# Attention stage of a four-stage layer: decayed scores become the stationary operand, values stream, and the residual is summed by tokens

## The chip, the cores and the metric

One core of a Trainium2 chip. The metric is the device time of the program in microseconds, as the median of its runs; lower is better. Each core has TensorE (PE, with its weight loads shown apart as PEld), VectorE (DVE), ScalarE (ACT), GpSimd (POOL) and SyncE (SP), which issues the DMAs.

## The reference, cut to what matters

Four residual steps over 1024 tokens (4 batches of 256) of 256 features: `x = x + A(layernorm(x))`, `x = x + FFN(layernorm(x))`, `x = x + B(layernorm(x))`, `x = x + FFN(layernorm(x))`. The change lies in B and in the two norms around it. B has 16 heads. For one head, with 128 key features and 256 value features:

```python
q = silu(group_conv(h @ Wq.T)); k = silu(group_conv(h @ Wk.T)); v = h @ Wv.T
beta = sigmoid(h @ Wb.T + bb); gate = sigmoid(h @ Wg.T + bg)
S_t = beta_t * S_(t-1) + k_t v_t^T          # scan over the 256 tokens of a batch
o_t = (q_t S_t) * gate_t
out = concat_over_heads(o) @ Wo.T
```

The scan equals a masked product within a batch: o = M V, with M[l, m] = (q_l . k_m) times a decay for m <= l, and zero otherwise.

## The kernel before, in words

All of it is one hand-ordered program: each engine has its own list of instructions, in program order, and waits on counting semaphores. x lies in SBUF by features: `x[p, k, token]`, 128 partitions of features, two feature halves k (KT = 2), 1024 tokens. The normed input `xn` has the same layout. Every product is made from pairs of fp32r parts, hi and lo, by `mm3` (L241 to L245): three matmuls into the same place of PSUM, w.hi v.hi, w.hi v.lo, w.lo v.hi, each with a weight load of its own. The hi part is a copy on ACT (L389), the lo part a subtraction on POOL (L393) or DVE.

A norm (`norm_pe`, `norm_act`, `norm_dve`) runs before each stage: means by a matmul of x with a constant matrix (L294), x minus mean on DVE (L376), squares on ACT, variances by matmuls (L301), the inverse root on DVE, its spread over partitions by a matmul (L310), the scaling on DVE and the hi/lo split. `keep_busy` (L316) issues matmuls of zeros so that PE doesn't fall silent.

Stage B (`b_pe`, `b_act`, `b_dve`, `b_pool`, `b_sp`) goes over 16 heads. The value and output weights are multiplied first ("fold"), so that a head's contribution to x is M (xn fold) and no output projection follows. While head h is finished, head h + 1 is made. PE's order in one head (`b_head_pe`): fold and the two projections of q and k of head h + 1; scores of batches 0 and 1; values of head h + 1 (8 blocks of tokens, 48 matmuls); **value product of batch 0**; scores of batches 2 and 3; **value product of batch 1**; the two convolutions of head h + 1 (72 matmuls); **value products of batches 2 and 3**. The last head makes nothing.

For one batch the score product s has keys m on partitions and queries l on columns; only three of its four 128x128 blocks are kept, as 384 columns (TRI): [keys 0, queries 0], [keys 1, queries 1], [keys 0, queries 1]. DVE bounds the exponents (L707), ACT takes the exponentials (L713, L714), DVE multiplies them with the scores (`b_score_dve`, m_b, L1496), ACT and POOL split the result into `ms_b` hi and lo. Then `b_value_pe` makes the head's part of x, by features:

```python
for d in range(KT):
    mm3(half_view(o[:, d*SEQ:(d+1)*SEQ]), v block 0 [:, dv], first_m(ms), ...)   # 256 columns
    mm3(o[:, d*SEQ+P:(d+1)*SEQ], v block 1 [:, dv], ms[:, P:2P], ...)            # 128 columns
```

The first argument after the output is the stationary operand, the second the moving one. `b_value_dve` adds the bank to x (L1502, 128x512). The PSUM banks: 6 and 7 for the value products, 4 and 5 for the scores, 3 for the fold, 0, 1, 2 and 4 for the convolutions. In the convolutions, PE's second one (s = 1) waits for DVE to have read the banks of the first (`b_conv_y`, L1471 to L1476), and DVE does so behind the last `m_b` of the head. In rows of the profile a matmul is named by its moving operand, then its stationary one: `ps<-ms_b_hi,vtok_hi` is a value product of before, with `vtok` stationary.

## Time and profile before

| | |
|---|---|
| median of 3 runs (lowest, highest) | 1497.19 us (1496.82, 1499.1) |
| the profiled execution | 1496.01 us |
| its span, first to last instruction | 1494.2 us |
| mean granted TensorE clock | 0.989 of full |
| PE busy, instructions | 1437.9 us (96%), x8520 |
| DVE, ACT, POOL busy | 897.2, 863.9, 817.1 us |
| stage B | about 703.8 us (first mean of its norm) to 1226.7 us (first mean of the next norm) |

How to read it: a timeline row gives start, duration, engine, line, operation, output<-inputs, partitions x columns and count, and in brackets how long the engine sat idle before it and what released it. A PE matmul's own duration includes its way through the array, so what a matmul costs in a stream is the distance from its start to the start of the next, called the pitch below.

### The profile page before, as it was taken

How to read it: one execution, taken by the hardware profiler on the slowest of the kernel's cores; microseconds unless marked ns; L12 is line 12 of the kernel's file. 1: busy time of each engine (PE TensorE's matmuls, PEld its weight loads, DVE VectorE, ACT ScalarE, POOL GpSimd, SP SyncE). 2: the span in 40 equal slices, each digit the busy share in tenths (PEclk: the TensorE clock that was granted, in tenths of full speed). 3: DMA queues.
4: the chain of work that ended last, by engine and by line, in shares of the span. 5: the costliest groups of instructions: out<-in, count | busy, mean ns of one | idle time of the engine just before them, and what ended most of it. 6: DMA issues, size and time to landing. Idle time of an engine off the chain costs nothing.

```text
span 1494.2 us, 24410 instructions
## 1 busy us (share of the span) xinstructions
PE 1437.9 (96%) x8520; PEld 1248.1 (84%) x8520; DVE 897.2 (60%) x1713; ACT 863.9 (58%) x1735; POOL 817.1 (55%) x685
## 2 busy tenths in 40 slices
PE   7799999999999999999999999999999999999998
PEld 5589898898976778887789999999999987778886
DVE  6776766767664443434766767677666754443434
ACT  5566666666655343333677777777777755343332
POOL 4744444444434555553576666766676634555553
PEclk9999999999999999999999999999999989999999
DMA  2133332332311111111232123212222011111111
GB/s 83 32 66 79 68 69 67 67 78 68 69 53 32 43 43 53 42 53 32 65 82 63 51 57 74 63 49 56 63 63 63 15 42 33 43 42 53 42 53 39
DMA packets 48603, 82.48 MB, mean 55 GB/s; under 512 B 4256, under 2 KB 29984, under 8 KB 48288
## 3 DMA queue, kind: packets, MB, share of 16 engines
q1 hardware_dynamic: 48544, 81.70, 21.1%
q8 instruction: 36, 0.59, 0.2%
q14 instruction: 23, 0.19, 0.0%
HBM read 80.38 MB, written 1.31 MB: 55 GB/s over the span
## 4 chain that ended last, share of the span: by engine, by line
PE 58%; issue 5%; ACT 5%; DVE 4%; POOL 4%; DMA 0%; DVEq 0%; POOLq 0%; ACTq 0%; SPq 0%
PE ps L243 19%; PE ps L245 18%; PE ps L244 18%; POOL planes_lo L393 1%; POOL ms_b_lo L393 1%; ACT q L1317 1%; POOL qk_lo L393 1%; PE ps L294 1%; PE ps L301 1%; DVE qsum L1455 1%; ACT planes_hi L1322 1%; DVE f_h L1081 0%; DMA fw_raw<-ffn_w 0%; ACT qk_hi L389 0%; ACT fh_hi L389 0%
## 5 line engine op out<-in xcount | busy, mean ns | idle before, releaser
L393 POOL TENSOR_TENSOR ms_a_lo<-m_a,ms_a_hi 128x384 fp32r<-128x384 f32 x128 | 129.9, 1015 | 200.2 <-ACT ms_a_hi L389 200.2
L1081 DVE TENSOR_TENSOR f_h<-f_sc,ps 128x512 f32<-128x512 f32 x112 | 76.4, 682 | 182.5 <-POOL f_sc L1013 182.5
L243 PE MATMUL ps<-xn_hi,fgu_hi 128*128 128x512 f32 x448 | 177.3, 396 | 5.2 <-DVE f_h L1081 5.2
L245 PE MATMUL ps<-xn_hi,fgu_lo 128*128 128x512 f32 x448 | 178.2, 398 | 0.0
L244 PE MATMUL ps<-xn_lo,fgu_hi 128*128 128x512 f32 x448 | 177.0, 395 | 0.0
L1083 DVE TENSOR_TENSOR fh_lo<-f_h,fh_hi 128x512 fp32r<-128x512 f32 x112 | 107.2, 957 | 98.3 <-ACT fh_hi L389 98.3
L962 ACT ACTIVATE f_s<-ps 128x512 f32<-128x512 f32 x112 | 66.7, 597 | 161.2 <-PE ps L245 161.0
L1013 POOL TENSOR_TENSOR f_sc<-f_s,coef_r 128x512 f32<-128x512 f32 x88 | 114.0, 1296 | 67.5 <-ACT f_s L962 67.5
L389 ACT CAST fh_hi<-f_h 128x512 fp32r<-128x512 f32 x112 | 69.1, 617 | 124.9 <-DVE f_h L1081 124.8
L393 POOL TENSOR_TENSOR fd_lo<-fw_raw,fd_hi 128x256 fp32r<-128x256 f32 x56 | 52.1, 930 | 125.7 <-ACT fd_hi L389 125.7
L243 PE MATMUL ps<-xn_hi,aw_hi 128*128 128x512 f32 x256 | 108.8, 425 | 7.4 <-DVE bmat_lo L696 7.4
L744 DVE TENSOR_TENSOR m_a<-ps,e_a 128x384 f32<-128x384 f32 x128 | 71.4, 558 | 63.5 <-ACT e_a L714 47.4
L393 POOL TENSOR_TENSOR ms_b_lo<-m_b,ms_b_hi 128x384 fp32r<-128x384 f32 x64 | 64.8, 1013 | 78.8 <-ACT ms_b_hi L389 78.8
L243 PEld LDWEIGHTS ps<-xn_hi,fgu_hi 128*128 128x128 f32 x448 | 84.3, 188 | 27.9 <-issue 6.0
L393 POOL TENSOR_TENSOR qk_lo<-qf,qk_hi 128x512 fp32r<-128x512 f32 x64 | 84.1, 1335 | 36.5 <-ACT qk_hi L389 36.5
L245 PE MATMUL ps<-xn_hi,aw_lo 128*128 128x512 f32 x256 | 102.0, 399 | 0.0
L244 PE MATMUL ps<-xn_lo,aw_hi 128*128 128x512 f32 x256 | 101.6, 397 | 0.0
L244 PEld LDWEIGHTS ps<-xn_lo,fgu_hi 128*128 128x128 f32 x448 | 84.1, 188 | 20.5
L245 PEld LDWEIGHTS ps<-xn_hi,fgu_lo 128*128 128x128 f32 x448 | 84.2, 188 | 20.1
L243 PE MATMUL ps<-fh_hi,fd_hi 128*128 128x512 f32 x224 | 89.0, 397 | 0.6 <-DVE fh_lo L1083 0.6
L244 PE MATMUL ps<-fh_lo,fd_hi 128*128 128x512 f32 x224 | 88.2, 394 | 0.0
L245 PE MATMUL ps<-fh_hi,fd_lo 128*128 128x512 f32 x224 | 87.2, 389 | 0.0
(276 smaller groups left out, 4901.1 us busy)
## 6 DMA issues: line engine op xcount, KB each, us to landing
fw_raw<-ffn_w SPq DMA_DIRECT2D x56, 384.0 KB, 3.0
rows_a<-a_rows_d SPq DMA_DIRECT2D x64, 256.0 KB, 4.8
wconv_raw<-b_conv SPq DMA_DIRECT2D x16, 513.0 KB, 3.6
aw_raw<-a_heads SPq DMA_DIRECT2D x32, 256.0 KB, 5.2
wvo_raw<-b_vo SPq DMA_DIRECT2D x16, 512.0 KB, 3.6
rows_b<-b_rows_d SPq DMA_DIRECT2D x32, 256.0 KB, 4.8
wqk_raw<-b_qk SPq DMA_DIRECT2D x16, 256.0 KB, 4.8
x<-xT SPq DMA_DIRECT2D x2, 512.0 KB, 4.9
```

What stands on the lines that cost most here:

```text
L243: nc.tensor.matmul(o, w[0], v[0], start=first, stop=False, skip_group_check=True)
L244: nc.tensor.matmul(o, w[0], v[1], start=False, stop=False, skip_group_check=True)
L245: return nc.tensor.matmul(o, w[1], v[0], start=False, stop=last, skip_group_check=True)
L294: ins = nc.tensor.matmul(ps[:, mean_bank(n) + c, :], mean_w[:], x[:, k, cols(c)], start=k == 0, stop=k == KT - 1)
L301: ins = nc.tensor.matmul(ps[:, 2 + c, i:i + 1], ln_sq[:, k, block_of(c, i)], mean_w[:, 0:1], start=k == 0 and i == 0, stop=k == KT - 1 and ...
L389: return nc.scalar.copy(dst[0], src).then_inc(sem(hi_sem), 1)
L393: return nc.gpsimd.tensor_tensor(dst[1], src, f32(dst[0]), ALU.subtract).then_inc(sem(done_sem), 1)
L744: nc.vector.tensor_tensor(m_a[:, u % 2, :], ps[:, 4 + u % 2, 0:TRI], e_a[:, u % 2, :], ALU.mult).then_inc(sem("a_m_done"), 1)
L962: nc.scalar.activation(f_s[:, c], ps[:, c, :], ACT.Silu).then_inc(sem("f_silu"), 1)
L1013: nc.gpsimd.tensor_tensor(f_sc[:, c], f_s[:, c], coef[:, cols(c)], ALU.mult).then_inc(sem("f_sc"), 1)
L1081: nc.vector.tensor_tensor(f_h[:, c], f_sc[:, c], ps[:, 2 + c, :], ALU.mult).then_inc(sem("f_h"), 1)
L1083: nc.vector.tensor_tensor(fh[1][:, p, cols(c)], f_h[:, c], f32(fh[0][:, p, cols(c)]), ALU.subtract).then_inc(sem("f_h_split"), 1)
```

## The change

In each of the 64 value products (16 heads, 4 batches) the operands change places: `ms_b` is stationary and `vtok` moves, 256 columns wide. The output then has tokens on partitions and features on columns, so one batch's part takes 3 `mm3` (9 matmuls of 256 columns) where it took 4 (6 of 256 columns and 6 of 128). x must have the same layout while it is summed. So within the norm ahead of stage B, after the means, PE turns x over: 4 batches of 4 transposes each into banks 4 to 7, and DVE copies batches 0 and 1 back over x, ACT batches 2 and 3. In the last head PE turns each batch back after its value product has been added (turn 0 ahead of value 2, turn 1 ahead of value 3, turns 2 and 3 behind it), and DVE copies each one back. `x_final` of the norm behind the stage waits for these copies (`x_turned`) where it waited for the additions. PE's zero matmuls in the norm ahead of stage B go to bank 0 instead of 4. Three semaphores are merged into others, with no change of order.

```diff
--- before.py
+++ after.py
@@ -273,11 +273,13 @@
         X_FINAL = {1: lambda c: 4 * A_TILES + 2 * c + 2, 2: lambda c: 2 * c + 2,
-                   3: lambda c: BATCH * (B_HEADS - 1) + 2 * c + 2, 4: lambda c: 2 * c + 2}
+                   4: lambda c: 2 * c + 2}
         def x_final(eng, n, c):
             if n == 0:
                 eng.wait_ge(sem(f"x_loaded{c}"), 16)
+            elif n == 3:
+                eng.wait_ge(sem("x_turned"), BATCH + 2 * c + 2)
             else:
                 eng.wait_ge(sem(f"x_updated{n}"), X_FINAL[n](c))
@@ -293,6 +295,9 @@
                 for k in range(KT):
                     ins = nc.tensor.matmul(ps[:, mean_bank(n) + c, :], mean_w[:], x[:, k, cols(c)], start=k == 0, stop=k == KT - 1)
                 ins.then_inc(sem("ln_mean"), 1)
+            if n == 2:
+                for b in range(BATCH):
+                    turn_pe(b, 4 + b).then_inc(sem("x_turn"), 1)
             for c in range(CHUNKS):
                 for k in range(KT):
@@ -302,18 +307,34 @@
                                                start=k == 0 and i == 0, stop=k == KT - 1 and i == CHUNK_BLOCKS - 1,
                                                skip_group_check=True)
                 ins.then_inc(sem("ln_var"), 1)
-                keep_busy(pe, (6, 3)[c])
-            pe.wait_ge(sem("ones_made"), 1)
+                keep_busy(pe, (6, 3)[c], 0 if n == 2 else 4)
+            pe.wait_ge(sem("mean_made"), 2)
             for c in range(CHUNKS):
                 pe.wait_ge(sem("ln_diag"), CHUNKS * n + c + 1)
                 nc.tensor.matmul(ps[:, 2 + c, :], ones_w[:], ln_diag[:, c, :], start=True, stop=True).then_inc(sem("ln_rstd"), 1)
-                keep_busy(pe, 3)
-        def keep_busy(pe, n):
+                keep_busy(pe, 3, 0 if n == 2 else 4)
+        def of_turn(b):
+            return x[:, :, b * SEQ:(b + 1) * SEQ]
+        def turn_pe(b, bank):
+            for i in range(2):
+                for k in range(KT):
+                    at_ = i * DM + k * P
+                    ins = nc.tensor.transpose(ps[:, bank, at_:at_ + P], of_turn(b)[:, k, i * P:(i + 1) * P], ident)
+            return ins
+        def turned(bank):
+            return ps[:, bank, :].rearrange("p (i m) -> p i m", i=2)
+        def keep_busy(pe, n, bank):
             for _ in range(n):
-                nc.tensor.matmul(ps[:, 4, :], zero_w[:], zero_x[:], start=True, stop=True)
+                nc.tensor.matmul(ps[:, bank, :], zero_w[:], zero_x[:], start=True, stop=True)
         def block_of(c, i):
             return slice(c * CHUNK + i * P, c * CHUNK + (i + 1) * P)
@@ -330,6 +351,11 @@
             for c in range(CHUNKS):
                 act.wait_ge(sem("ln_v"), CHUNKS * n + c + 1)
                 nc.scalar.activation(norm_cols(ln_s, c), norm_cols(ln_v, c), ACT.Sqrt).then_inc(sem("ln_std"), 1)
+            if n == 2:
+                for b in range(2, BATCH):
+                    act.wait_ge(sem("x_turn"), b + 1)
+                    act.wait_ge(sem("ln_xc"), KT * CHUNKS * (n + 1))
+                    nc.scalar.copy(of_turn(b), turned(4 + b)).then_inc(sem("x_turned"), 1)
             for c in range(CHUNKS):
                 for k in range(KT):
                     act.wait_ge(sem("ln_xn"), KT * (CHUNKS * n + c) + k + 1)
@@ -375,6 +401,11 @@
                 for k in range(KT):
                     nc.vector.tensor_tensor(ln_xc[:, k, cols(c)], x[:, k, cols(c)], ps[:, mean_bank(n) + c, :],
                                             ALU.subtract).then_inc(sem("ln_xc"), 1)
+            if n == 2:
+                dve.wait_ge(sem("ln_xc"), KT * (CHUNKS * n + 1))
+                for b in range(2):
+                    dve.wait_ge(sem("x_turn"), b + 1)
+                    nc.vector.tensor_copy(of_turn(b), turned(4 + b)).then_inc(sem("x_turned"), 1)
             rstd(0)
             rstd(1)
             for c in range(CHUNKS):
@@ -808,8 +839,8 @@
                 sp.dma_start(aw_raw[:, h], a_heads[h * P:(h + 1) * P, :]).then_inc(sem(f"aw_loaded{h}"), 16)
             sp.dma_start(awo_raw[:], a_wo[0:P, :]).then_inc(sem("awo_loaded"), 16)
             sp.wait_ge(sem("a_cum"), 1)
-            sp.dma_start(a_rows_d, dec_e[:]).then_inc(sem("a_rows_stored"), 16)
-            sp.wait_ge(sem("a_rows_stored"), 16)
+            sp.dma_start(a_rows_d, dec_e[:]).then_inc(sem("rows_stored"), 16)
+            sp.wait_ge(sem("rows_stored"), 16)
             for c in range(CHUNKS):
                 sp.dma_start(rows_a[:, c], rows_of(a_rows_d, 0, c)).then_inc(sem(f"a_rows_loaded{c}"), 16)
             for g in range(A_TILES):
@@ -1096,6 +1127,7 @@
         def b_pe(pe):
             pe.wait_ge(sem("b_bg_w"), 1)
+            pe.wait_ge(sem("x_turned"), BATCH)
             for c in range(CHUNKS):
                 normed(pe, 2, c)
                 for s in range(2):
@@ -1239,13 +1271,10 @@
             elif not last:
                 pe.wait_ge(sem("v_split"), 4 * h + 5 + b)
             o, ms = ps[:, 6 + u, :], at(ms_b, slice(None), u)
-            for d in range(KT):
-                dv = slice(d * P, (d + 1) * P)
-                mm3(half_view(o[:, d * SEQ:(d + 1) * SEQ]), at(vtok[p], slice(None), 2 * b, dv), tuple(first_m(v) for v in ms),
-                    d == 0, False)
-                ins = mm3(o[:, d * SEQ + P:(d + 1) * SEQ], at(vtok[p], slice(None), 2 * b + 1, dv),
-                          at(ms, slice(None), slice(P, 2 * P)), False, d == KT - 1)
-            ins.then_inc(sem("b_o_done"), 1)
+            v0, v1 = (at(vtok[p], slice(None), 2 * b + i) for i in range(2))
+            mm3(o[:, 0:DM], at(ms, slice(None), slice(0, P)), v0, True, False)
+            mm3(o[:, DM:], at(ms, slice(None), slice(2 * P, TRI)), v0, False, False)
+            mm3(o[:, DM:], at(ms, slice(None), slice(P, 2 * P)), v1, False).then_inc(sem("b_o_done"), 1)
         def b_head_pe(pe, h, p, last):
             make = (lambda *parts: None) if last else (lambda *parts: b_make_pe(pe, h + 1, 1 - p, parts))
@@ -1258,8 +1287,15 @@
             b_score_pe(pe, h, p, 3, last)
             b_value_pe(pe, h, p, 1, last)
             make("conv0", "conv1")
+            if last:
+                b_turn_pe(pe, 0)
             b_value_pe(pe, h, p, 2, last)
+            if last:
+                b_turn_pe(pe, 1)
             b_value_pe(pe, h, p, 3, last)
+            if last:
+                b_turn_pe(pe, 2)
+                b_turn_pe(pe, 3)
         def b_prepare_act(act):
             act.wait_ge(sem("wbg_loaded"), 16)
@@ -1498,9 +1534,16 @@
         def b_value_dve(dve, h, b):
             dve.wait_ge(sem("b_o_done"), BATCH * h + b + 1)
-            at_ = (slice(None), slice(None), slice(b * SEQ, (b + 1) * SEQ))
-            nc.vector.tensor_tensor(x[at_], x[at_], ps[:, 6 + b % 2, :].rearrange("p (d l) -> p d l", d=KT),
-                                    ALU.add).then_inc(sem("x_updated3"), 1)
+            nc.vector.tensor_tensor(of_turn(b), of_turn(b), turned(6 + b % 2), ALU.add).then_inc(sem("x_updated3"), 1)
+        def b_turn_pe(pe, b):
+            pe.wait_ge(sem("x_updated3"), BATCH * (B_HEADS - 1) + b + 1)
+            turn_pe(b, b).then_inc(sem("x_turn"), 1)
+        def b_turn_dve(dve, b):
+            dve.wait_ge(sem("x_turn"), BATCH + b + 1)
+            nc.vector.tensor_copy(of_turn(b), turned(b)).then_inc(sem("x_turned"), 1)
         def b_head_dve(dve, h, p, last):
             make = (lambda *parts: None) if last else (lambda *parts: b_make_dve(dve, h + 1, 1 - p, parts))
@@ -1522,8 +1565,15 @@
             make("conv0")
             b_value_dve(dve, h, 1)
             make("conv1")
+            if last:
+                b_turn_dve(dve, 0)
             b_value_dve(dve, h, 2)
+            if last:
+                b_turn_dve(dve, 1)
             b_value_dve(dve, h, 3)
+            if last:
+                b_turn_dve(dve, 2)
+                b_turn_dve(dve, 3)
         def b_pool(pool):
             split_lo(pool, at(wbg, slice(None)), wbg_raw[:], "wbg_hi", 1, "b_bg_w")
@@ -1605,8 +1655,8 @@
                 sp.wait_ge(sem(f"{name}_split"), 1)
                 sp.dma_start(raw[:], src[P:2 * P, :]).then_inc(sem(f"{name}_loaded"), 16)
             sp.wait_ge(sem("b_row"), 1)
-            sp.dma_start(b_rows_d, bg_z[:, 1]).then_inc(sem("b_rows_stored"), 16)
-            sp.wait_ge(sem("b_rows_stored"), 16)
+            sp.dma_start(b_rows_d, bg_z[:, 1]).then_inc(sem("rows_stored"), 16)
+            sp.wait_ge(sem("rows_stored"), 32)
             for c in range(CHUNKS):
                 sp.dma_start(rows_b[:, c], rows_of(b_rows_d, 0, c)).then_inc(sem(f"b_rows_loaded{c}"), 16)
             with sp.Fori(0, B_HEADS - 2) as h:
@@ -1659,7 +1709,7 @@
         @block.vector
         def _(dve):
             nc.vector.memset(mean_w[:], 1.0 / DM).then_inc(sem("mean_made"), 1)
-            nc.vector.memset(ones_w[:], 1.0).then_inc(sem("ones_made"), 1)
+            nc.vector.memset(ones_w[:], 1.0).then_inc(sem("mean_made"), 1)
             a_early_dve(dve)
             dve.wait_ge(sem("consts_loaded"), 16)
             nc.vector.memset(zero_w[:], 0.0)
```

## Rows read from the trace of the kernel before

**Rows 1.** The page, part 1: busy time, share of the span and instructions of each engine.

```profile
PE 1437.9 (96%) x8520; PEld 1248.1 (84%) x8520; DVE 897.2 (60%) x1713; ACT 863.9 (58%) x1735; POOL 817.1 (55%) x685
```

**Rows 2.** Windows: stretch, length, busy (count) by engine, granted clock, DMA share, GB/s.

```profile
827.00:858.00 31.00, 30.27 (x230) 28.96 (x231) 21.81 (x47) 23.68 (x46) 20.74 (x17) 1.00 0.22 59
...
718.00:720.00 2.00, 2.00 (x6) 1.58 (x6) 2.00 (x2) 1.38 (x2) 2.00 (x2) 0.53 0.02 6
...
1216.00:1218.00 2.00, 2.00 (x11) 2.00 (x11) 0.00 (x0) 0.42 (x1) 1.00 (x1) 0.50 0.00 0
```

**Rows 3.** The chain of waits, 844 to 858: start, us, what.

```profile
847.32 0.59 ACT q L1317
...
855.43 0.57 DVE m_b L1496
...
856.61 1.02 POOL ms_b_lo L393
```

**Rows 4.** Timeline of PE: the first value product of two heads following each other.

```profile
827.10 0.38 PE L243 MATMUL ps<-ms_b_hi,vtok_hi 128*128 128x256 f32 x1 [0.64 <-POOL ms_b_lo L393]
...
857.75 0.38 PE L243 MATMUL ps<-ms_b_hi,vtok_hi 128*128 128x256 f32 x1 [0.64 <-POOL ms_b_lo L393]
```

**Rows 5.** Timeline of PE, 840 to 845: value products, then the fold.

```profile
840.76 0.33 PE L243 MATMUL ps<-ms_b_hi,vtok_hi 128*128 128x256 f32 x1
...
841.17 0.22 PE L243 MATMUL ps<-ms_b_hi,vtok_hi 128*128 128x128 f32 x1
841.23 0.28 PE L244 MATMUL ps<-ms_b_lo,vtok_hi 128*128 128x128 f32 x1
...
841.45 0.34 PE L243 MATMUL ps<-ms_b_hi,vtok_hi 128*128 128x256 f32 x1
...
842.84 0.34 PE L243 MATMUL ps<-wvo_hi 128*128 128x256 f32 x1
...
844.31 0.40 PE L243 MATMUL ps<-xn_hi,wqk_hi 128*128 128x512 f32 x1
```

**Rows 6.** Timeline of DVE and of PE, 832 to 836, the first convolution.

```profile
832.80 0.56 DVE L1496 TENSOR_TENSOR m_b<-ps,e_b 128x384 f32<-128x384 f32 x1 [1.25 <-ACT e_b L714]
833.78 0.43 DVE L1471 COPY conv_y<-ps 128x256 f32<-128x256 f32 x1 [0.42 <-PE ps L245]
...
835.04 0.42 DVE L1476 TENSOR_TENSOR conv_y<-conv_y,ps 128x256 f32<-128x256 f32 x1
...
835.72 0.28 PE L243 MATMUL ps<-planes_hi,wconv_hi 128*128 128x260 f32 x1
```

**Rows 7.** Timeline of ACT, 844 to 848.

```profile
844.51 0.59 ACT L1309 CAST fold_hi<-ps 128x512 fp32r<-128x512 f32 x1 [0.18 <-PE ps L245]
...
847.32 0.59 ACT L1317 COPY q<-ps 128x512 f32<-128x512 f32 x1 [0.69 <-PE ps L245]
```

**Rows 8.** Timeline of PE, 66 to 67: eight transposes of an earlier stage.

```profile
66.07 1.06 PE L491 MATMUL ps<-const,stage 128*128 128x128 f32 x8
66.89 0.48 PE L243 MATMUL ps<-xn_hi,aw_hi 128*128 128x512 f32 x1
```

**Rows 9.** Timeline of ACT and of PE, the norm ahead of stage B.

```profile
714.63 1.21 ACT L336 CAST xn_hi<-ln_xc 128x512 fp32r<-128x512 f32 x2 [2.16 <-DVE ln_xc L364]
...
717.77 0.50 PE L243 MATMUL ps<-xn_hi,wbg_hi 128*128 128x512 f32 x1 [1.94 <-POOL wbg_lo L393]
```

**Rows 10.** Timeline of PE and DVE, the last head and the norm behind it.

```profile
1212.26 0.36 PE L243 MATMUL ps<-qk_hi 128*128 128x256 f32 x1 [1.82 <-POOL qk_lo L393]
...
1215.73 0.58 PE L243 MATMUL ps<-ms_b_hi,vtok_hi 128*128 128x256 f32 x1 [1.37 <-POOL ms_b_lo L393]
...
1225.31 0.39 PE L243 MATMUL ps<-ms_b_hi,vtok_hi 128*128 128x256 f32 x1 [0.37 <-POOL ms_b_lo L393]
...
1226.73 3.65 PE L294 MATMUL ps<-x,mean_w 128*128 128x512 f32 x8
1226.94 0.69 DVE L1502 TENSOR_TENSOR x<-x,ps 128x512 f32<-128x512 f32 x1 [1.27 <-PE ps L245]
```

## The prediction

> **What bounds the kernel now.** The page's busy times come first: PE is busy for 96% of the span and its weight loads for 84%, every other engine for at most 60% [rows 1]. A window over one head of stage B shows the same at full clock: PE 30.27 of 31 us, the weight loads 28.96, ACT 23.68 [rows 2]. Then the waits of PE. In this stage the one that comes back in every head stands ahead of the first value product, 0.64 us, released by the lo split of `ms_b` on POOL [rows 4]; the heads follow each other at 857.75 - 827.10 = 30.65 us. 14 such waits are there (the last of them 0.47 us, the others 0.63 or 0.64).
>
> A wait of 0.64 us doesn't say that POOL bounds the head, so the chain of waits is read next [rows 3]. From the first value product (827.10) to the end of the first q projection (about 847.3) the chain is PE alone. There it goes over to ACT (847.32), and through ACT, DVE and POOL by turns until POOL's split at 856.61, which releases PE. This second part, 847.32 to 857.75 = 10.43 us, is a latency that PE's work beside it (projections, scores, values) doesn't fill. So a head is 20.2 us bound by PE and 10.4 us bound by a round trip. What the reader must check is where the changed matmuls lie. All four value products of a head lie between its first one and the next fold, so all lie in PE's part.
>
> **The value products.** In the stream of before, 840.76 to 841.45 is half a batch: three matmuls of 256 columns and three of 128, 0.69 us [rows 5]. The first of the narrow ones has a pitch of 0.06, the other two 0.11, and the next wide one 0.17 where a wide one costs 0.118 otherwise: the fold's twelve take 844.31 - 842.84 = 1.47, less the 0.17 of the first, over eleven. So narrow matmuls cost (0.69 - 3 x 0.118) / 3 = 0.112 us each, almost as much as the wide ones: half the columns buy nothing, since the weight load sets the pace of a narrow matmul and only just not that of a wide one. The change keeps the columns (6 x 256 + 6 x 128 = 9 x 256 = 2304) and drops 3 of 12 weight loads. A batch falls from 2 x 0.69 = 1.38 to 9 x 0.118 = 1.06 us, so by 0.32, and a head by 1.28. Bounds: 1.38 - 9 x 0.112 = 0.37 saved if the narrow price held for all, and 6 x 0.118 + 6 x 0.06 - 1.06 = 0 if columns alone counted. I take 0.32, since the new stream is of the fold's shape, a measured row. DVE's addition keeps its shape, 128x512 from one bank, 0.69 us [rows 10].
>
> The Trainium skill, in TensorE: Matmul & The Clock Gate, section Back-to-back issue gap, gives about 81 ns for a matmul of 128 columns within a stream of weight loads and matmuls. By that a batch of before would be 6 x 0.118 + 6 x 0.081 = 1.19 us and the saving 0.13. The rows say 0.112, and they decide.
>
> **What comes late next in a head.** Seen from the first value product, batch 0 and 1 bring the convolutions 0.64 us earlier. DVE reads the first convolution's bank at 833.78 after an idle 0.42, behind `m_b` of batch 3, which ends at 832.80 + 0.56 = 833.36 [rows 6]. That `m_b` hangs on the exponents and DVE's own order, not on PE's value products (DVE is still in its value splits when product 0 is done), so it stays put. The read moves by 0.36 and not by 0.64; it ends at 835.46 - 0.36 = 835.10. PE would be at its second convolution at 835.72 - 0.64 = 835.08, and with the way of a semaphore it starts near 835.2: 0.1 lost. The second half of the convolutions has more room. Then value products 2 and 3 bring a further 0.64. On ACT the q copy that heads the chain at 847.32 sat idle for 0.69 before [rows 7]. ACT itself moves forward by about 0.55 (it follows DVE's last read) and 0.18 (the wait at 844.51). So 1.15 - 0.73 = 0.42 of the 0.69 is used and the copy is still released by PE. The 10.43 us behind it keep their length, and the wait of 0.64 stays as it is. A head saves 1.28 - 0.13 = 1.15 us. Bounds: 1.28 with no loss, 0.73 if ACT were to hold the copy back by all that the rows leave open.
>
> The 14 distances between first value products (head 0 to head 14) give 14 x 1.15 = **-16.1**. In head 14 products 0 and 1 still count, and 2 and 3 vanish in a wait: PE stands for 1.82 us ahead of the last head's scores [rows 10], released by a split that hangs on DVE's convolution read. That is **-0.5**.
>
> **The last head.** The clock is at half from about 1213 to 1223 [rows 2, 10], so a value product costs 2.6 us and saves 0.64. Product 0 is on the chain (DVE adds it before it makes the exponents of batches 2 and 3), product 1 too (the split of batch 3 waits until it has been read). That is **-1.3**. Bounds: -0.6 at full clock, -1.3 at half.
>
> **Turning x over ahead of the stage.** 16 transposes stand on PE between the means and the variances. Eight such ones, of the same type and shape, take 66.89 - 66.07 = 0.82 us, 0.103 each [rows 8]: 16 x 0.103 = 1.65. PE had no wait between means and variances, and the variances, the zero matmuls and the spread follow on PE in order, so all of it counts: **+1.7**. Bounds: 1.65 and, at half clock, 3.3. The copies: two on DVE at about 0.69 (the addition reads a bank of the same size), while DVE waits for the variances, which come 1.7 later; two on ACT at about 0.59 (as its q copy), in an idle of 2.16 [rows 9]. I take them as free. Without that cover they would cost 1.4 and 1.2. PE's new wait for the copies ahead of the gate product is long over at 717.77 + 1.7.
>
> **Turning it back.** Behind the last value product, PE was free for the means at once: 1226.73, 3.5 us for both. Now it makes turn 2, waits for DVE's last addition (0.2 + 0.69 behind the product), makes turn 3 and only then the means: 0.95 + 0.1 + 4 x 0.103 = 1.45 later. DVE's copy of batch 3 is hidden by the first mean (1.7 us). Turns 0 and 1 stand ahead of products 2 and 3: 0.4 each, 0.8 at half clock, of which the wait of 0.37 ahead of the last product [rows 10] takes a part. I take 0.9 (bounds 0.4 and 1.6). Together **+2.4**, bounds 1.8 and 3.1.
>
> **The sum**, from the profiled execution's own 1496.01 (1.8 above its span): -16.1 - 0.5 - 1.3 + 1.7 + 2.4 = -13.8, so 1482.2. The median of the runs shown is 1.2 above that execution, so 1483.4 is the forecast. DMA isn't touched: the three merged semaphores keep their order, and the weights of a head are needed 1.15 us earlier each, against landing times of a few us within a head of 29.5. With the bounds put together, 14 x 1.28 and the low ends give 1480.5, 14 x 0.73 and the high ends 1491.5.
>
> **Rivals.**
>
> A. *The round trip holds.* If ACT or DVE, not PE, releases the q copy after the change, only part of each head's 1.28 counts and the wait ahead of the first product grows instead. For it: ACT is busy for 23.68 of 31 us [rows 2] and has 0.27 left by my count. Against: the idle of 0.69 is there. At 0.73 a head the sum is 1496.01 - 10.2 + 2.3 = 1488.1, with the offset 1489.3. Chance 0.12.
>
> B. *Narrow matmuls weren't dear.* Half of the saving is an artefact of modelled starts, or the new stream is slower than the fold's. With 0.13 a batch, 0.4 a head after the convolution loss, 14 heads give 5.6, head 14 0.1, the last head 0.5, against 4.1 for the turns: 1496.0 - 2.1 + 1.2 = 1495.1. With no saving at all it is 1497.2 + 4.1 = 1501.3. Against it stand the starts themselves, which add up to the distance between heads, so no time is modelled away. This is the case in which the change doesn't do what it says. Chance 0.04, of which 0.01 with no gain at all. The skill's figure of 81 ns would lead here.
>
> C. *The clock falls at the seams.* The rows show falls after PE was thin or idle: an idle of 1.94 at 717.77 and then 0.53 of the clock [rows 2, 9], 1.82 at 1212.26 and then 0.50 for 10 us. If transposes count as such idleness, the norm ahead of the stage (14 us of PE, some of it paced by DVE) runs at half: about +5, and the means behind it (3.5 becoming 7) about +3: 1483.4 + 8 = 1491. Against: after the eight transposes at 66.07 the matmuls have full pitch, and the 15 us in which they'd lie are at 1.00 now. The skill says in TensorE: Matmul & The Clock Gate, Part 4: PE-mode transpose, that a transpose isn't counted as activity by the clock's gate; the rows have no stretch of transposes long enough to show it. Chance 0.08.
>
> D. *Slower.* The wait ahead of the first product grows to 0.64 + 1.15 = 1.8 us because the whole round trip, from the previous head's DVE work on, is what sets the head. Then no time is won, and the wait is as long as those of 1.82 and 1.94 that were followed by a half clock; at 717.77 that lasted for 3.5 us. At the shortest, each head loses 1.7 us in such a spell: 1496 + 14 x 1.7 + 4 + 1.2 = 1525. It decides from a wait of about 1.8 us on; the waits of 0.64 leave the clock at 1.00 [rows 2, 4]. Against: the chain shows PE alone ahead of 847.32. Chance 0.03.
>
> **Chances and range.** The forecast has 0.73, and its own range is 1480.5 to 1486.5. To hold 8 in 10 the range reaches to A: 1480 to 1489.5. About 0.2% (3 us) is what a measurement of this kernel can tell from no change. Faster by more than that: the forecast, A and C, 0.93; within it the larger part of B, 0.03; slower D and the rest of B, 0.04.
>
> **What would show it.** Distance between first value products 29.5 us (before 30.65), and the wait ahead of them still near 0.64. A batch of value products 1.06 us from its first matmul to the next operation, nine matmuls with a pitch of 0.118 and `vtok` named first. A wait or a gap of about 0.1 on PE at the start of the second convolution. PE instructions 8520 - 64 x 3 + 32 = 8360. 16 transposes in about 1.7 us behind the first means, and the gate product 1.7 later relative to them. Means behind the stage starting about 1.5 us after the last value product. Wrong it would be if the distance between heads were above 30 us, if the wait ahead of the first product were above 1 us, or if the granted clock fell inside the heads.

## The result, and the profile after

The changed kernel takes 1482.57 us, median of 4 runs (1481.42 to 1482.94); the kernel before, on the same chip, 1497.01 (1495.96 to 1499.1). The ratio is 0.9903 with a 95% interval of 0.9891 to 0.9914: about 14 us faster, where 1483.4 was forecast. The profiled execution took 1482.8 with a span of 1481.0, so the spans differ by 13.2.

The page of the changed kernel, its first line of busy times; it answers to [rows 1]:

```profile
PE 1420.5 (96%) x8354; PEld 1228.3 (83%) x8360; DVE 901.3 (61%) x1719; ACT 861.7 (58%) x1737; POOL 819.8 (55%) x685
```

The 8360 instructions that were counted ahead are there as weight loads (PEld), one for each matmul; six matmul records are missing from the trace. PE loses 17.4 us of busy time and stays at 96%. The copies that turn x over and back are DVE's six and ACT's two more instructions.

The timeline of PE in the changed kernel: the first batch of one head and the scores behind it; then the first product of the next head; it answers to [rows 4, 5]:

```profile
826.90 0.38 PE L243 MATMUL ps<-vtok_hi,ms_b_hi 128*128 128x256 f32 x1 [0.79 <-POOL ms_b_lo L424]
827.12 0.28 PE L244 MATMUL ps<-vtok_lo,ms_b_hi 128*128 128x256 f32 x1
...
827.93 0.28 PE L245 MATMUL ps<-vtok_hi,ms_b_lo 128*128 128x256 f32 x1
828.05 0.28 PE L243 MATMUL ps<-qk_hi 128*128 128x256 f32 x1
...
856.54 0.38 PE L243 MATMUL ps<-vtok_hi,ms_b_hi 128*128 128x256 f32 x1 [0.80 <-POOL ms_b_lo L424]
```

A batch is nine matmuls. The first of a head takes 828.05 - 826.90 = 1.15 us (its first matmul comes out of a wait and has a pitch of 0.22), where it took 1.43. The last two of the head take 839.38 to 841.48 = 2.10 together, where they took 2.72. The wait ahead of the first product has grown from 0.64 to 0.80, and that was not forecast. The distance between heads is 29.61 on the mean of fourteen, where it was 30.62.

The same spans, put into a ledger between events that both traces have (us, before, after, difference; it adds up to the 13.2). A gate product is the first product behind the norm ahead of the stage, a router product the first behind the next norm:

```
                                             before   after    diff   forecast
start -> first mean ahead of the stage       703.76  704.51   +0.75   0
first mean -> gate product                    14.01   15.75   +1.74   +1.7
gate product -> first value product, head 0   48.07   47.41   -0.66   0
heads 0 to 14 (14 distances)                 428.69  414.61  -14.08   -16.1
head 14 -> first mean behind the stage        32.20   31.61   -0.59   +0.6
first mean -> router product                  14.06   14.01   -0.05   0
the rest                                     253.41  253.10   -0.31   0
```

The first row is nothing of the change: over the profiled executions of all kernels here, which run the same work up to there, it lies between 703.64 and 705.79. So the total times of single kernels scatter by some 2 us ahead of the stage alone, and the ledger's rows within the stage say more than the totals.

### The profile page after: what moved, and what is told of

Its sections match the earlier page's. It is cut to its first block and busy times, and to the rows that moved or that the text cites. A ratio compares the mean times of both kernels' runs of the same rounds, so it can differ in the third digit from the quotient of the medians.

```text
span 1481.0 us, 24095 instructions
## 1 busy us (share of the span) xinstructions
PE 1420.5 (96%) x8354; PEld 1228.3 (83%) x8360; DVE 901.3 (61%) x1719; ACT 861.7 (58%) x1737; POOL 819.8 (55%) x685
```

## The experiments

### The two halves of the change apart

One kernel has the new value products and no turns. The value matmuls are those of the change, everything else is the kernel before:

```diff
-            for d in range(KT):
-                dv = slice(d * P, (d + 1) * P)
-                mm3(half_view(o[:, d * SEQ:(d + 1) * SEQ]), at(vtok[p], slice(None), 2 * b, dv), tuple(first_m(v) for v in ms),
-                    d == 0, False)
...
+            mm3(o[:, 0:DM], at(ms, slice(None), slice(0, P)), v0, True, False)
+            mm3(o[:, DM:], at(ms, slice(None), slice(2 * P, TRI)), v0, False, False)
+            mm3(o[:, DM:], at(ms, slice(None), slice(P, 2 * P)), v1, False).then_inc(sem("b_o_done"), 1)
```

> The value products turned round as in the change, x left by features as before (the sum over heads then mixes features and tokens): what the products give without the price of the turns. Theory (16 transposes on PE's path ahead of the stage, two turns inside the last head and two behind it, all paid): the change less 1.7 ahead of the stage and less about 2.1 at its end, 1482.6 - 3.8 = 1478.8 us; distance between heads 29.63 us as in the change. Rival 1 (the turns are hidden by the waits around them): 1482.6. Rival 2 (transposes pull the clock down): more than 6 us below the change.

Measured: 1480.75 us (1480.53 to 1480.99), ratio to the kernel before 0.9892 [0.9875, 0.9908]. The distance between heads is 29.61 and the wait 0.80, as in the change, so both belong to the products and neither to the turns. Its last head, timeline of PE from the last value product to the first mean:

```profile
1210.82 0.39 PE L243 MATMUL ps<-vtok_hi,ms_b_hi 128*128 128x256 f32 x1 [0.47 <-POOL ms_b_lo L393]
...
1211.99 1.02 PE L294 MATMUL ps<-x,mean_w 128*128 128x512 f32 x2
```

From head 14's first product to the mean it takes 30.18, the change 31.61: turning back costs 1.43. From the first value product of the last head to the mean it takes 9.57 against 11.00 before, so the cheaper products save 1.43 there (forecast 1.3). The expectation of 1478.8 was missed by 2 us: it had turns of 3.8, and between the two traces they are 1.74 + 1.43 = 3.2; 1.15 more lies ahead of the stage, where this execution came late (705.66 for 704.51).

The other kernel has the turns and the old products (the same diff the other way round, on the changed kernel).

> The reverse: x is turned over and back, the value products stay as before (the sum mixes features and tokens): the price of the turns alone. Theory: 1497.0 + 1.7 + 2.1 to 2.4 = 1500.9 us, distance between heads 30.63 us, and the gate product about 1.7 us later behind the first mean. Rival 1 (hidden): 1497.0. Rival 2 (clock): over 1503, with a granted clock below 1 in the norm.

Measured: 1499.73 (1498.53 to 1502.1), ratio 1.0023 [1.0013, 1.0032], so +3.3 us with the turns alone. The distance between heads is 30.62 and the wait 0.64, those of before. The gate product comes 15.75 behind the first mean, the 1.74 of the change. From the last head's first value product to the mean it takes 1229.55 - 1217.72 = 11.83, against 11.00 before. So turning back costs 0.83 beside the old products and 1.43 beside the new ones; no run shows why the two differ.

### Does the weight load set the price?

Each wide matmul of the change is cut into two of 128 columns: the same columns, twice the matmuls and weight loads.

```diff
-            mm3(o[:, 0:DM], at(ms, slice(None), slice(0, P)), v0, True, False)
...
+            for d in range(KT):
+                dv = slice(d * P, (d + 1) * P)
+                w0, w1 = at(v0, slice(None), dv), at(v1, slice(None), dv)
+                mm3(o[:, d * P:(d + 1) * P], at(ms, slice(None), slice(0, P)), w0, d == 0, False)
...
```

> The change with each of its 9 matmuls of 256 columns cut into two of 128: the same 2304 columns in a batch, 18 weight loads for 9. Theory (a matmul of 128 columns costs 0.112 us because its weight load sets the pace): a batch 18 x 0.112 = 2.02 for 1.06, 0.96 more; 58 batches lie on PE's part of the heads, so +56, with the last head's two at half clock +58: about 1540 us. Rival 1 (columns set the time): 1482.6 to 1486. Rival 2 (0.081 us for such a matmul, the figure of the Trainium skill): 18 x 0.081 = 1.46, +0.40 x 58 = +23: 1506 us.

Measured: 1548.05 (1547.58 to 1549.68), ratio 1.0344 [1.0327, 1.0361]. One batch in its timeline of PE, the first matmul, the fourth and the last, and the scores behind it:

```profile
834.45 0.32 PE L243 MATMUL ps<-vtok_hi,ms_b_hi 128*128 128x128 f32 x1 [0.63 <-POOL ms_b_lo L424]
...
834.83 0.28 PE L243 MATMUL ps<-vtok_hi,ms_b_hi 128*128 128x128 f32 x1
...
836.40 0.28 PE L245 MATMUL ps<-vtok_hi,ms_b_lo 128*128 128x128 f32 x1
836.51 0.33 PE L243 MATMUL ps<-qk_hi 128*128 128x256 f32 x1
```

Eighteen matmuls take 2.06 us, with a pitch of 0.11 where no neighbour is wide. Nine more matmuls with their weight loads and no more columns cost 2.06 - 1.15 = 0.91 a batch, and a head grew by 3.55 (33.16 for 29.61). So rival B is out: narrow matmuls are as dear as the rows of before had them. Still narrower ones cost almost the same. In the changed kernel, sixteen matmuls of a single column (of fp32, where the products are of fp32r) in the norm take 714.39 - 712.69 = 1.70 us, 0.106 each (timeline of PE):

```profile
712.69 1.84 PE L306 MATMUL ps<-mean_w,ln_sq 128*128 128x1 f32 x16
714.39 0.81 PE L337 MATMUL ps<-zero_x,zero_w 128*128 128x512 bf16 x3
```

So up to 128 columns it isn't the columns that are paid for. That it is the weight load, and not a fixed price of any matmul, is argued and not shown: every matmul of these kernels has a weight load of its own, and no kernel here drops one without the other.

The kernel came out 8 us above the 1540 that were expected. 14 heads make 49.6 of some 66 us; some 10 of the rest lie in the last head, at half clock. The window over the last head, the turns and the way to the means in this kernel (columns as in rows 2: length, busy by engine, granted clock, DMA share, GB/s):

```profile
1252.00:1278.00 26.00, 24.93 (x112) 23.59 (x112) 9.31 (x19) 6.16 (x14) 4.42 (x5) 0.50 0.00 1
```

PE is busy for 24.93 of 26 us at half clock. The same part, from the last head's first value product to the first mean, takes 1276.49 - 1255.09 = 21.4 here and 11.0 in the change.

### Where is a microsecond of PE worth a microsecond?

The forecast split a head into a part bound by PE and a part bound by a round trip. Two kernels put the same three matmuls on zeros (0.65 us, three of 512 columns) into the one part and into the other.

```diff
+            if not last:
+                keep_busy(pe, 3, FOLD_BANK)
             b_value_pe(pe, h, p, 2, last)      # in PE's part
...
+            if not last:
+                keep_busy(pe, 3, FOLD_BANK)
             b_value_pe(pe, h, p, 0, last)      # in the round trip's part
```

> The change with three matmuls of zeros (3 x 0.215 = 0.65 us) ahead of the value product of batch 2 in heads 0 to 14, that is in the part of the head in which the chain of waits is PE alone. Theory (what is added or taken there counts in full): 14 heads x 0.65 = +9.0, 1491.6 us; distance between heads 30.28; the wait ahead of the first value product unchanged or some 0.1 shorter. Rival (the round trip through ACT, DVE and POOL sets the head): under +3, with the wait shrinking by what is added.

> The change with three matmuls of zeros (0.65 us) ahead of the value product of batch 0 in heads 0 to 14, that is in the part of the head in which the chain goes through ACT, DVE and POOL and PE ends up waiting 0.79. Theory (PE's work there is hidden up to the length of the wait): the wait falls to about 0.15, the distance between heads stays 29.6, time as the change, a ratio to before of 0.990 to 0.991. Rival (PE's time counts wherever it stands): +9 us, 1491.

Measured: in PE's part 1490.24 (1489.39 to 1491.83), ratio 0.9954 [0.9937, 0.997]; the 14 distances are 421.05, so 6.44 longer, 0.46 a head. In the round trip's part 1484.13 (1482.07 to 1484.54), ratio 0.9911 [0.9895, 0.9928], distance 29.61: nothing. The second kernel's timeline of PE shows where the zeros went:

```profile
855.46 0.38 PE L337 MATMUL ps<-zero_x,zero_w 128*128 128x512 bf16 x1
...
855.98 0.38 PE L243 MATMUL ps<-vtok_hi,ms_b_hi 128*128 128x256 f32 x1
```

They fill the wait, of which 0 to 0.18 is left. The split of the head holds: what is added ahead of the first value product is hidden, and what is added ahead of the third is paid. But in PE's part 0.65 cost only 0.46, since the wait went back from 0.79 to 0.63. From the timeline of PE of the first kernel, the first product of two heads:

```profile
829.04 0.38 PE L243 MATMUL ps<-vtok_hi,ms_b_hi 128*128 128x256 f32 x1 [0.63 <-POOL ms_b_lo L424]
...
859.12 0.38 PE L243 MATMUL ps<-vtok_hi,ms_b_hi 128*128 128x256 f32 x1 [0.64 <-POOL ms_b_lo L424]
```

So the 0.16 that the change adds to the wait goes away when PE's part is made longer again. What meets what on the other engines is the next question.

### Who made the wait longer?

The timeline of DVE and of POOL in the changed kernel, at the head of the round trip:

```profile
847.07 0.87 DVE L1494 TENSOR_TENSOR planes_lo<-q,planes_hi 128x512 fp32r<-128x512 f32 x1 [0.83 <-ACT planes_hi L1358]
...
848.65 0.68 DVE L1494 TENSOR_TENSOR planes_lo<-q,planes_hi 128x512 fp32r<-128x512 f32 x1
```

```profile
844.67 2.73 POOL L424 TENSOR_TENSOR qk_lo<-qf,qk_hi 128x512 fp32r<-128x512 f32 x2
847.42 1.02 POOL L424 TENSOR_TENSOR planes_lo<-qsum,planes_hi 128x256 fp32r<-128x256 f32 x1
```

And in the kernel before:

```profile
848.46 0.69 DVE L1458 TENSOR_TENSOR planes_lo<-q,planes_hi 128x512 fp32r<-128x512 f32 x1 [1.19 <-ACT planes_hi L1322]
...
849.85 0.68 DVE L1458 TENSOR_TENSOR planes_lo<-q,planes_hi 128x512 fp32r<-128x512 f32 x1
```

```profile
845.70 2.72 POOL L393 TENSOR_TENSOR qk_lo<-qf,qk_hi 128x512 fp32r<-128x512 f32 x2 [0.54 <-ACT qk_hi L389]
848.81 0.84 POOL L393 TENSOR_TENSOR planes_lo<-qsum,planes_hi 128x256 fp32r<-128x256 f32 x1 [0.39 <-ACT planes_hi L1324]
```

Before, POOL was done with the lo splits of k (848.42) when DVE began its first split of the planes (848.46). After the change q comes 1.4 us sooner and POOL's splits only 1.0: they end at 847.40, and DVE's split at 847.07 runs beside them. It takes 0.87 instead of 0.69, and all behind it on DVE is 0.18 late (from split to split 1.58 instead of 1.39). The theory: POOL beside it makes DVE slow, so POOL must be done with k sooner. Three kernels test it. The first takes a large split off POOL's way to k (the lo split of the next head's window sums, which stands ahead of k in POOL's order):

```diff
-            if name == "wconv":
+            if name == "wconv" and isinstance(h, int) and h < 2:
...
                 b_weights_pool(pool, "wvo", h + 2, p)
+                b_wsum_lo_pool(pool, h + 2, p)
```

> The change, with one of POOL's jobs in a head (the lo split of the summed convolution weights, 1.3 us) moved from behind the large weight split to an idle stretch ahead of it, so that the lo split of k (2.7 us) can start earlier; nothing else is moved. Theory (the wait ahead of the first value product grew from 0.64 to 0.79 because that split of k now runs beside DVE's first instructions of the round trip, which last 0.87 instead of 0.69 us beside it): k's split is then released by ACT at about 0.1 us earlier, so only a part of the overlap goes: wait 0.70 to 0.79, time 1481.0 to 1482.5. Rival (the growth comes from ACT's or PE's own chain): wait and time unchanged, 1482.5.

Measured: 1482.94 (1481.71 to 1484.46), ratio 0.9905 [0.9889, 0.9922], to be held against the changed kernel itself, run on the same chip:

> The changed kernel itself, once more, on the chip on which the next three run: 1482.5 us, a ratio to before of 0.990, distance between heads 29.63 us and the wait ahead of the first value product 0.79.

It gave 1484.11 (1482.29 to 1485.81), ratio 0.9909 [0.9892, 0.9926]. The distance (29.61) and the wait (0.80) are the same in both: a miss, as POOL was not what k waited for any more. The timeline of POOL, early in the stage, shows why:

```profile
815.20 2.73 POOL L424 TENSOR_TENSOR qk_lo<-qf,qk_hi 128x512 fp32r<-128x512 f32 x2 [1.23 <-ACT qk_hi L420]
```

POOL now stands idle for 1.23 us until ACT has cast k, and its splits end as late as in the change (0.31 to 0.34 behind DVE's start). So ACT's order is the next thing: k's casts ahead of the fold's.

```diff
+                b_k_hi_act(act, h, p)
                 make("fold")
-                b_k_hi_act(act, h, p)
```

> The same, and on ACT the hi parts of k are made ahead of the copy of the fold, so that POOL can begin k's lo split about 0.5 us earlier and has left DVE alone when the round trip starts. Theory: DVE's first split of the round trip back to 0.69 us, wait back to about 0.64, distance between heads 29.48, 14 x 0.15 = 2.1 us less than the change: 1480.4. Rival: no gain, 1482.5, or a loss since the fold's lo part and DVE's sum of the planes come 0.3 to 0.5 us later: up to 1489.

> Only the move on ACT: the hi parts of k ahead of the copy of the fold, POOL's order as in the change. Theory (what stretched the round trip is POOL's split of k running beside DVE's first instruction of it): POOL is still busy with its weight splits until about 0.7 us after the hi part of k is there, so its split of k starts and ends as late as in the change, DVE's split still takes 0.87 us, wait 0.79, distance between heads 29.6, time as the change: a ratio of 0.990 to 0.991. Rival (the gain came from ACT's order itself): wait 0.61, distance 29.44, 0.989.

With both edits: 1481.06 (1479.35 to 1482.24), ratio 0.9889 [0.9872, 0.9905], distance 29.43, wait 0.59 to 0.63. The interval overlaps that of the changed kernel on this chip, so it is the distances that decide. Its timelines of POOL and of DVE:

```profile
843.84 2.55 POOL L424 TENSOR_TENSOR qk_lo<-qf,qk_hi 128x512 fp32r<-128x512 f32 x2 [0.76 <-ACT qk_hi L420]
```

```profile
846.71 0.69 DVE L1494 TENSOR_TENSOR planes_lo<-q,planes_hi 128x512 fp32r<-128x512 f32 x1
```

POOL ends at 846.39, ahead of DVE's 846.71, and DVE is back at 0.69. With ACT's order alone 1483.94 (1481.2 to 1484.54), ratio 0.9905 [0.9888, 0.9923], distance 29.60, wait 0.74 to 0.82:

```profile
846.72 0.90 DVE L1494 TENSOR_TENSOR planes_lo<-q,planes_hi 128x512 fp32r<-128x512 f32 x1 [0.81 <-ACT planes_hi L1358]
```

```profile
844.30 2.76 POOL L424 TENSOR_TENSOR qk_lo<-qf,qk_hi 128x512 fp32r<-128x512 f32 x2
```

POOL's splits end at 847.06 here, behind DVE's start, and DVE takes 0.90. Only where the overlap is gone is the 0.18 gone. All thirteen traces here (before, the change and the eleven runs) agree, over fourteen heads each. In seven (the change, its repeat, no turns, the early split, ACT's order alone, zeros in the round trip, zeros in the last head) POOL's splits end 0.29 to 0.37 us behind DVE's start, and DVE takes 0.85 to 0.92. In the six others (before, the turns alone, the halves, zeros in PE's part, both edits, all moves together) POOL is done first, and DVE takes 0.69.

### The clock in the last head

[rows 2, 10] showed half a clock in the last head. The changed kernel has it too, only earlier, at 1200 and not at 1213. One kernel fills PE's waits there with matmuls on zeros (2.43 ahead of the scores, 1.10 ahead of the values):

```diff
+            if last:
+                keep_busy(pe, 11, FOLD_BANK)
             b_score_pe(pe, h, p, 0, last)
             b_score_pe(pe, h, p, 1, last)
             make("values")
+            if last:
+                keep_busy(pe, 6, FOLD_BANK)
```

> The change with matmuls of zeros in the two waits of PE in the last head (11 ahead of its first scores, 2.4 us; 6 ahead of its first value product, 1.3 us). In the change the clock is at half there from 1200 to about 1207. Theory (the idle of 2.43 brings the fall): no fall, the first value product 1.06 instead of 2.09 and what hangs on it earlier, 1 to 2 us less: 1481.0. Rival (the fall comes from something else, or the zeros stand in the way of the scores): 1482.5 to 1483.5, clock still at half.

Measured: 1483.18 (1482.36 to 1484.84), ratio 0.991 [0.9893, 0.9926]. The windows in the changed kernel, then in this one:

```profile
1200.00:1202.00 2.00, 1.78 (x9) 1.59 (x8) 0.56 (x1) 1.31 (x5) 0.66 (x2) 0.50 0.03 8
1206.00:1208.00 2.00, 2.00 (x16) 2.00 (x16) 1.48 (x5) 0.88 (x3) 0.00 (x0) 0.82 0.00 0
```

```profile
1200.00:1202.00 2.00, 2.00 (x15) 1.66 (x16) 0.56 (x1) 1.30 (x5) 1.06 (x1) 1.00 0.03 8
1206.00:1208.00 2.00, 1.62 (x14) 1.38 (x13) 1.06 (x3) 1.30 (x4) 0.00 (x0) 1.00 0.00 0
```

The clock stays full, as the expectation had it, but the gain is at its low end. From head 14 to the mean it takes 30.68 against 31.61, so -0.9, which is less than the runs can tell apart in the whole time: half a clock for 7 us costs little where PE then waits for POOL (1.43 us ahead of the third value product here, 0.65 in the change).

The two gains together (three moves) give the lowest time of this study:

> The change with the three moves together: the lo split of the summed weights early on POOL, the hi parts of k ahead of the fold's copy on ACT, zeros in PE's waits of the last head. Theory (each takes away what it took away alone): distance between heads 29.44 us for 29.61, 14 x 0.18 = 2.5 less, and 0.9 less in the last head: 3.4 us less than the change, a ratio to before of 0.9875, about 1479 to 1480 us. Rival (the gains overlap or one was scatter): 1481 to 1482.

Measured: 1479.67 (1478.72 to 1480.0), ratio to the kernel before 0.988 [0.9863, 0.9896]; distance 29.42, head 14 to the mean 30.63. By its trace that is 2.72 in the 14 distances and 0.98 behind them, 3.7 below the change. By the medians it is 2.9, on different chips, and the intervals of the two ratios overlap.

## Why the prediction was right

**The sum.** -13.8 was forecast between two profiled executions, -13.2 it was. Four things were off, and they cancel, so that the sum comes this close is in part luck: heads +2.0 against the forecast, the end of the stage -1.2, the way from the gate to the first value product -0.7, and what lies outside the change +0.4. The bounds that the prediction names, put together, give 1481.0 and 1492.3, not 1480.5 and 1491.5; its range doesn't hang on that.

**The value products: right.** 1.25 us a head by the traces of one head (product 0 0.28, product 1 with the scores ahead of it 0.32, products 2 and 3 0.62, the fold 0.03) against 1.28, from four batches at 9 x 0.118. The halves kernel shows the cause: 0.91 a batch for nine more matmuls with their weight loads. The Trainium skill, TensorE: Matmul & The Clock Gate, section Back-to-back issue gap, gives about 81 ns for a matmul of 128 columns in such a stream. By that an estimate for the eighteen is 18 x 0.081 = 1.46 us; 2.06 was measured, so here the measurement decides.

**The convolutions: nearly right.** 0.1 was to be lost, 0.06 was. The timeline of DVE in the changed kernel:

```profile
832.62 0.56 DVE L1532 TENSOR_TENSOR m_b<-ps,e_b 128x384 f32<-128x384 f32 x1 [1.25 <-ACT e_b L745]
833.09 0.41 DVE L1507 COPY conv_y<-ps 128x256 f32<-128x256 f32 x1
```

As reckoned, `m_b` doesn't move against the start of the head (5.72 behind it, 5.70 before), and the read stands right behind it, without the idle 0.42 of [rows 6].

**The round trip: the step that failed.** The forecast said "The 10.43 us behind it keep their length, and the wait of 0.64 stays as it is." It is 10.61 (845.93 to 856.54). The start was right: PE, not ACT, still releases the q copy, with 0.34 of idle left where 0.27 was reckoned. The timeline of ACT:

```profile
845.93 0.59 ACT L1353 COPY q<-ps 128x512 f32<-128x512 f32 x1 [0.34 <-PE ps L245]
```

But a chain that keeps its instructions doesn't keep their durations when it moves against another engine's work. POOL's splits of k had 0.04 us of room before the change, and the forecast hadn't looked at POOL, as it isn't on that part of the chain. So the distance fell by 1.00 and not by 1.15: PE's part shortened by 1.25 - 0.06 = 1.19, and 0.18 came back in the round trip. 14 x 0.15 = 2.1 is the whole miss of the heads (2.0 by the ledger). No rival had this: A had ACT or DVE holding the copy back, and that didn't happen.

**The last head: products right, turns too dear.** The new products gave 1.43 (forecast 1.3) and head 14 gave 0.6 (forecast 0.5). The turns cost 1.43, not 2.4. The timeline of PE in the changed kernel, the last products with the turns between them:

```profile
1208.23 0.60 PE L328 MATMUL ps<-const,x 128*128 128x128 f32 x4
1209.48 0.39 PE L243 MATMUL ps<-vtok_hi,ms_b_hi 128*128 128x256 f32 x1 [0.65 <-POOL ms_b_lo L424]
...
1210.64 0.60 PE L328 MATMUL ps<-const,x 128*128 128x128 f32 x4
1211.29 0.39 PE L243 MATMUL ps<-vtok_hi,ms_b_hi 128*128 128x256 f32 x1
...
1212.45 0.60 PE L328 MATMUL ps<-const,x 128*128 128x128 f32 x4
1213.39 0.66 PE L328 MATMUL ps<-const,x 128*128 128x128 f32 x4 [0.34 <-DVE x L1537]
1213.89 1.02 PE L296 MATMUL ps<-x,mean_w 128*128 128x512 f32 x2
```

Behind the last value product it is as forecast: 1213.89 - 1212.45 = 1.44 with the wait for DVE between (1.45 reckoned). Turn 0 ends at about 1208.8 and PE still waits 0.65 for the split; turn 1 took the place of the wait ahead of the last product, which without the turns is 0.47. So the 0.9 allowed for both is 0: that term was mis-sized, and it is where the -1.2 at the end of the stage comes from, with 0.2 from the products. The half clock that the allowance was for had come and gone by then.

**Ahead of the stage: right.** 16 transposes cost 1.74 (forecast 1.65, taken as 1.7). The timeline of PE, the transposes and the variances behind them:

```profile
707.95 1.91 PE L328 MATMUL ps<-const,x 128*128 128x128 f32 x16
709.69 1.84 PE L306 MATMUL ps<-mean_w,ln_sq 128*128 128x1 f32 x16
```

That the copies are free holds too, as nothing but this 1.74 came on top.

**Rival C: the other way round.** The window over the gate products of the changed kernel; in the kernel before, that stretch had a fall of the clock [rows 2, 9]:

```profile
720.00:724.00 4.00, 3.29 (x13) 2.41 (x14) 3.91 (x8) 2.43 (x5) 4.00 (x4) 1.00 0.26 66
```

The wait of 1.94 is still there, yet the clock stays at 1.00, and from the gate product to the fold it takes 6.42 us instead of 7.24. That is 0.8 won. Behind the fold 0.16 of it is lost again: to the first value product of head 0 it takes 40.99 instead of 40.83. Both traces have a second fall of the clock there, at about 756 to 760. The windows over it in the changed kernel, and in the one with zeros in the last head, which has the same instructions up to there:

```profile
756.00:760.00 4.00, 3.98 (x10) 3.14 (x11) 3.24 (x4) 2.69 (x6) 3.20 (x4) 0.57 0.14 53
```

```profile
756.00:760.00 4.00, 2.81 (x12) 2.31 (x13) 2.75 (x4) 2.97 (x7) 3.75 (x3) 1.00 0.40 145
```

The second has no fall and takes 40.25, 0.74 less (46.66 from its gate product, where the ledger has 47.41). So a fall can come in one execution and stay away in another with the same instructions before it, and the ledger's -0.66 could as well have been -1.4. The products alone have the first fall, the turns alone don't (the windows of these two, columns as above: granted clock 0.67 and 1.00):

```profile
719.00:723.00 4.00, 3.33 (x9) 2.68 (x10) 3.91 (x4) 2.17 (x3) 4.00 (x4) 0.67 0.28 69
```

```profile
721.00:725.00 4.00, 3.39 (x13) 2.47 (x14) 3.91 (x8) 2.43 (x5) 4.00 (x4) 1.00 0.23 66
```

In the profiled executions of all ten kernels with transposes ahead of it the first fall is absent; in the two without, it is there. The Trainium skill, TensorE: Matmul & The Clock Gate, Part 4: PE-mode transpose, says that a transpose doesn't count as PE being busy in the same way as a matmul. If that held for these, it would speak for a fall in the norm, and no run here had one there. Why the first fall is gone with the transposes, by their activity, by moving the wait or, with one execution of each kernel, in part by chance, isn't settled: no kernel here put other work, or an equal delay, in their place.

**Rival D** (slower, from a wait of 1.8 us) was far off: the wait is 0.80, and the granted clock within the heads is 1.00.

## What to carry to other kernels

Where a narrow matmul costs almost as much as one twice as wide, count matmuls with their weight loads, not columns: three of twelve dropped gave 0.3 us a batch with the columns unchanged. A gain on the path moves two engines against each other, so look beside the chain too: which instruction of DVE and which of POOL had just missed each other, and what is the new distance. Price an added step by the wait that stands ahead of the next instruction, not by its length.

## What the hardware showed unexpectedly

- DVE's subtraction of two SBUF operands (128x512) takes 0.69 us when POOL's is done before it starts. When it starts 0.29 to 0.37 us before POOL's is done it takes 0.85 to 0.92, and it ends 0.54 to 0.57 us behind POOL's end in each of the 98 heads. In the first head of the kernel before, the overlap is longer (timelines of DVE and of POOL):

```profile
755.35 1.28 DVE L1458 TENSOR_TENSOR planes_lo<-q,planes_hi 128x512 fp32r<-128x512 f32 x1 [0.41 <-ACT planes_hi L1322]
```

```profile
753.38 2.70 POOL L393 TENSOR_TENSOR qk_lo<-qf,qk_hi 128x512 fp32r<-128x512 f32 x2 [0.41 <-ACT qk_hi L389]
```

POOL ends at 756.08, 0.73 behind DVE's start, and DVE at 756.63, again 0.55 behind POOL. So DVE's length is the overlap and 0.55 us more. The Trainium skill, SBUF — State Buffer, section SBUF: two separate sides, says that DVE and GpSimd lock a port pair against each other for such instructions, the loser blocked altogether. The traces agree: DVE's end follows POOL's. That it loses only 0.18 to 0.21 of an overlap of 0.33 would mean, as an estimate from 0.69 - 0.55, that about the first 0.14 us of the instruction aren't held up.
- In the halves kernel the clock stayed at half for 26 us with PE busy for 24.93 of them with loads and narrow matmuls; it came back only among the means. In the changed kernel it came back within 7 us, between the first and the second value product of the last head (the window over 1206 to 1208 above). No run shows what makes the difference.
